# Self-attention of a decoder layer: value products of 130 columns, the output in five pieces, and one 16-bit copy of the exponentials made by VectorE

## The reference

```python
qn = _rmsnorm(q, q_gamma) * dh ** (-0.5)
kn = _rmsnorm(k, k_gamma)
sim = jnp.einsum('bhid,bhjd->bhij', qn, kn)
attn = jax.nn.softmax(sim, axis=-1)
out = jnp.einsum('bhij,bhjd->bhid', attn, v)
```

## Time and profile before

| what | value |
| --- | --- |
| runs, us | 2266.23, 2267.96, 2263.83; median 2266.23 |
| the profiled execution's own time | 2270.32 us |
| its span, first to last instruction | 2268.5 us |
| mean granted TensorE clock | 0.989 |
| instructions | 62703, of them 22392 matmuls |
| DMA | 65.24 MB in 102349 packets |

### The profile page before, as it was taken

One profiled execution on the slowest core, in us unless ns is written; L12 is line 12 of the kernel. 1 busy time (PEld: TensorE's weight loads), 2 busy tenths in 40 slices (PEclk: granted clock), 3 DMA queues, 4 the chain that ended last, 5 costly groups with the idle time before them and its releaser, 6 DMA issues. The chain is left out here.

```text
span 2268.5 us, 62703 instructions
## 1 busy us (share of the span) xinstructions
PE 2161.2 (95%) x22392; PEld 1243.8 (55%) x22392; DVE 1567.6 (69%) x2601; ACT 1606.2 (71%) x1831; POOL 1451.5 (64%) x1010
## 2 busy tenths in 40 slices
PE   6999999999997999999999999999999978998999
PEld 3545666666664455444445456666666644554444
DVE  6997777777776666753379977777777766677522
ACT  4557999999997566631146489999999965666210
POOL 3425889888887586721234178889888975866210
PEclk9999999999999999999999999999999999999999
DMA  5210000000002202102122100000000031020000
GB/s 108 65 42 1 11 0 9 9 9 9 9 9 63 64 2 48 38 21 73 43 63 64 28 2 10 9 0 9 9 9 9 10 89 38 2 62 24 20 24 33
DMA packets 102349, 65.24 MB, mean 29 GB/s; under 512 B 75346, under 2 KB 75346, under 8 KB 102226
## 3 DMA queue, kind: packets, MB, share of 16 engines
q1 hardware_dynamic: 102226, 63.57, 12.7%
HBM read 46.69 MB, written 8.39 MB: 24 GB/s over the span
## 5 line engine op out<-in xcount | busy, mean ns | idle before, releaser
L599 POOL TENSOR_TENSOR qkn<-wide 128x1024 f16<-128x1024 f32 x448 | 952.9, 2155 | 140.2 <-PE bank L716 124.1
L920 DVE TENSOR_REDUCE sq<-bank 128x1 f32<-128x512 f32 x1024 | 685.3, 688 | 216.3 <-PE bank L668 209.7
L845 ACT ACTIVATE wide<-bank,shift 128x1024 f32<-128x1024 f32 x512 | 571.4, 1116 | 14.5 <-POOL qkn L599 6.5
L837 ACT ACTIVATE wide<-bank,shift 128x1024 f16<-128x1024 f32 x512 | 569.1, 1112 | 9.1 <-PE bank L684 9.1
L683 PE MATMUL bank<-q_hh,ko 128*128 (+1 forms) x1024 | 388.7, 380 | 13.1 <-ACT wide L845 13.0
L668 PE MATMUL bank<-ko,q_hh 128*128 (+1 forms) x1024 | 386.8, 380 | 9.2 <-DVE sq L920 5.9
L684 PE MATMUL bank<-q_lm,k_h 65*128 (+1 forms) x1024 | 389.0, 380 | 0.0
L701 PEld LDWEIGHTS bank<-v_hl,wide 128*128 128x128 f16 x4096 | 287.6, 98 | 63.3 <-issue 5.6
L701 PE MATMUL bank<-v_hl,wide 128*128 (+1 forms) x4096 | 319.8, 192 | 0.1
L703 PE MATMUL bank<-v_hl,wide 128*128 (+1 forms) x4096 | 318.2, 193 | 0.0
L703 PEld LDWEIGHTS bank<-v_hl,wide 128*128 128x128 f16 x4096 | 267.5, 96 | 58.7
(11 more groups left out here) (227 smaller groups left out, 4177.4 us busy)
## 6 DMA issues: line engine op xcount, KB each, us to landing
wide<-in_x SPq DMA_DIRECT2D x32, 256.0 KB, 2.7
q_lm<-in_x SPq DMA_DIRECT2D x32, 256.0 KB, 3.2
ko<-in_L_ffn_W SPq DMA_DIRECT2D x32, 256.0 KB, 4.0
q_hh<-q_hh SPq DMA_DIRECT2D x32, 128.0 KB, 2.6
ko<-k_h SPq DMA_DIRECT2D x32, 128.0 KB, 2.8
out<-bo_b SPq DMA_DIRECT2D x16, 256.0 KB, 2.0
out<-xbo_b SPq DMA_DIRECT2D x16, 256.0 KB, 2.0
q_lm<-sq SPq DMA_DIRECT2D x248, 0.2 KB, 4.9
```

The lines of the kernel that those rows point to most:

```text
L599: pool.tensor_tensor(probs_l[:, p % 2, :], probs[:, p % 2, :], probs_h[:, p % 4, :], ALU.subtract).then_inc(pl_pool, 1)
L837: act.activation(probs_h[:, p % 4, :], SB[p % 2][:, :], ACT.Exp, bias=shift[:, 0:1]).then_inc(ph_ready, 1)
L845: act.activation(probs[:, p % 2, :], SB[p % 2][:, :], ACT.Exp, bias=shift[:, 0:1]).then_inc(p_ready, 1)
L920: dve.tensor_reduce(pm[:, s, k:k + 1], MB[k % 2], AX_X, ALU.max).then_inc(mx_free, 1)
```

## The change

It has three parts. (1) `values_high`: for three of the four query groups the products of 65 and of 64 columns become one of 130 columns; the spare column is filled with ones too, and a unit's result takes 3 x 130 + 65 columns of its bank: the part from the low columns of V stands beside the part from the high ones. The fourth group stays as it was. (2) `output`: in five steps, one behind each of the maxima 4 to 8. Step 0 is the reciprocal, step 1 the multiplication of the four high parts, steps 2 to 4 add, for one query group each, the low part times the reciprocal. (3) For pair 6, ACT makes the 32-bit exponential alone; VectorE makes `probs_h` from it by a `tensor_reduce` with maximum over an axis of one element, behind maximum 11 (behind number 9 in the first unit), and TensorE's high products and POOL's subtraction of that pair wait for it on a semaphore of its own, `ph_dve`. Left out below are the lines that make the semaphores `ph_dve` and `o_high`.

```diff
@@ -494,6 +496,8 @@
                     LA = 2
                     MAXED = UNITS - LA
                     AHEAD = 6
+                    CAST = 6
+                    WIDE = TPC - 1
                     vf = v_hl
                     next_h = {"o": share4[0], "xq": share4[1]}
                     next_l = {"o": share4[2], "xq": share4[3]}
@@ -584,7 +588,7 @@
 
                         pool.wait_ge(a_v_done, T0 + KB)
                         pool.nop(nofuse=True)
-                        pool.memset(v_hl[:, :].rearrange("p (k e) -> p k e", e=VW)[:, :, DH:DH + 1], 1.0)\
+                        pool.memset(v_hl[:, :].rearrange("p (k e) -> p k e", e=VW)[:, :, DH:DH + 2], 1.0)\
                             .then_inc(a_ones, 1)
                         pool.wait_ge(a_ones, (b + 1) * (KB + 1))
                         pool.nop(nofuse=True)
@@ -594,6 +598,10 @@
                                 if p == DVE_PAIR:
                                     continue
                                 pool.wait_ge(p_ready, G + p + 1)
+                                if p == CAST:
+
+                                    pool.wait_ge(ph_dve, U0 + u + 1)
+                                    pool.nop(nofuse=True)
 
                                 pool.wait_ge(lo_done, G + p + 1)
                                 pool.tensor_tensor(probs_l[:, p % 2, :], probs[:, p % 2, :], probs_h[:, p % 4, :],
@@ -685,7 +693,10 @@
                             mm.then_inc(s_ready, 1)
 
                         def values_high(u, p, ob):
-                            pe.wait_ge(ph_ready, (U0 + u) * PAIRS + p + 1)
+                            if p == CAST:
+                                pe.wait_ge(ph_dve, U0 + u + 1)
+                            else:
+                                pe.wait_ge(ph_ready, (U0 + u) * (PAIRS - 1) + (p if p < CAST else p - 1) + 1)
                             if isinstance(u, int) and u == 0 and p == 0:
 
                                 pe.wait_ge(a_v_ready, T0 + KB + 1)
@@ -697,11 +708,13 @@
                                 v0 = (2 * p + half) * (H * VW) + u // CH * VW
                                 for t in range(TPC):
                                     rows = probs_h[:, p % 4, half * CT + t * P:half * CT + t * P + P]
-                                    o0 = t * (DH + 1)
-                                    pe.matmul(ob[:, o0:o0 + DH + 1], rows, vf[:, bass.ds(v0, DH + 1)],
+                                    o0 = t * VW
+                                    wide = VW if t < WIDE else DH + 1
+                                    pe.matmul(ob[:, o0:o0 + wide], rows, vf[:, bass.ds(v0, wide)],
                                               start=(p == 0 and half == 0 and t == 0), stop=False, skip_group_check=True)
-                                    pe.matmul(ob[:, o0:o0 + DH], rows, vf[:, bass.ds(v0 + DH + 2, DH)],
-                                              start=False, stop=False, skip_group_check=True)
+                                    if t >= WIDE:
+                                        pe.matmul(ob[:, o0:o0 + DH], rows, vf[:, bass.ds(v0 + DH + 2, DH)],
+                                                  start=False, stop=False, skip_group_check=True)
 
                         def values_low(u, p, ob):
 
@@ -834,7 +847,9 @@
                             G = (U0 + u) * PAIRS
                             for p in range(PAIRS):
                                 act.wait_ge(s_ready, G + p + 1)
-                                act.activation(probs_h[:, p % 4, :], SB[p % 2][:, :], ACT.Exp, bias=shift[:, 0:1]).then_inc(ph_ready, 1)
+                                if p != CAST:
+                                    act.activation(probs_h[:, p % 4, :], SB[p % 2][:, :], ACT.Exp, bias=shift[:, 0:1])\
+                                        .then_inc(ph_ready, 1)
 
                                 if p - 2 == DVE_PAIR:
                                     act.wait_ge(pl_dve, U0 + u + 1)
@@ -926,6 +941,12 @@
                             dve.tensor_reduce(nm0[:, :, DH] if isinstance(r, int) and r == 0 else nm[:, s, :], pm[:, s, :].rearrange("p (a k) -> p a k", k=4), AX_X, ALU.max,
                                               negate=True).then_inc(nm_ready, 1)
 
+                        def probs_high(u):
+                            p = CAST
+                            dve.wait_ge(p_ready, (U0 + u) * PAIRS + p + 1)
+                            dve.tensor_reduce(probs_h[:, p % 4, :], probs[:, p % 2, :].rearrange("p (n a) -> p n a", a=1), AX_X,
+                                              ALU.max).then_inc(ph_dve, 1)
+
                         def probs_low(u):
                             p, G = DVE_PAIR, (U0 + u) * PAIRS + DVE_PAIR
                             dve.wait_ge(p_ready, G + 1)
@@ -938,15 +959,28 @@
                             first = u // (2 * CH) * (CH * TPC * P) + u % CH * (TPC * P) + u // CH % 2 * DH
                             return of[:, bass.ds(first, TPC * P)].rearrange("p (t d) -> p t d", d=P)[:, :, 0:DH]
 
-                        def output(u, s):
-
-                            o4 = OB[s][:, 0:TPC * (DH + 1)].rearrange("p (t e) -> p t e", e=DH + 1)
+                        def output(u, s, step):
+
+                            skip = s * (TPC * VW - CT)
+                            four = pairs[3][:, s * CT - skip:s * CT - skip + TPC * VW].rearrange("p (t e) -> p t e", e=VW)
                             r4 = rden[:, :].rearrange("p (t a) -> p t a", a=1)
-                            dve.wait_ge(lo_done, (U0 + u + 1) * PAIRS + 2)
-                            dve.reciprocal(r4, o4[:, :, DH:DH + 1]).then_inc(o_rec, 1)
-                            dve.wait_ge(o_rec, U0 + u + 1)
-                            dve.tensor_tensor(o_out(u), o4[:, :, 0:DH], r4.broadcast_to([P, TPC, DH]), ALU.mult)\
-                                .then_inc(o_free, 1)
+                            o_u = o_out(u)
+                            if step == 0:
+                                dve.wait_ge(lo_done, (U0 + u + 1) * PAIRS + 2)
+                                dve.reciprocal(r4, four[:, :, skip + DH:skip + DH + 1]).then_inc(o_rec, 1)
+                            elif step == 1:
+                                dve.wait_ge(o_rec, U0 + u + 1)
+                                dve.tensor_tensor(o_u, four[:, :, skip:skip + DH], r4.broadcast_to([P, TPC, DH]), ALU.mult)\
+                                    .then_inc(o_high, 1)
+                            else:
+                                t = step - 2
+                                if t == 0:
+                                    dve.wait_ge(o_high, U0 + u + 1)
+                                low = dve.scalar_tensor_tensor(
+                                    out=o_u[:, t, :], in0=OB[s][:, t * VW + DH + 2:(t + 1) * VW], scalar=rden[:, t:t + 1],
+                                    in1=o_u[:, t, :], op0=ALU.mult, op1=ALU.add)
+                                if t == WIDE - 1:
+                                    low.then_inc(o_free, 1)
 
                         def split_both(pieces):
 
@@ -966,10 +1000,12 @@
                             for k in range(16):
                                 if maxed:
                                     reduce_max(u + LA, k, s)
-                                if k == 4 and not first:
-                                    output(u - 1, 1 - s)
+                                if 4 <= k < 4 + 2 + WIDE and not first:
+                                    output(u - 1, 1 - s, k - 4)
                                 if k == (6 if first else 2 * DVE_PAIR + 1):
                                     probs_low(u)
+                                if k == (9 if first else 2 * CAST - 1):
+                                    probs_high(u)
                             if maxed:
                                 negate_max(u + LA, s)
 
@@ -994,7 +1030,8 @@
                         split_both(PIECES_P3[0:2])
                         unit(MAXED + 1, 1, maxed=False)
                         split_both(PIECES_P3[2:4])
-                        output(UNITS - 1, 1)
+                        for step in range(2 + WIDE):
+                            output(UNITS - 1, 1, step)
 
 
             with ExitStack() as mlp:
```

More of the change, by code:

```diff
@@ L227, in decoder_layer @@
         ph_ready = sem("ph_ready")
+        ph_dve = sem("ph_dve")
         p_ready = sem("p_ready")
@@ L236, in decoder_layer @@
         o_rec = sem("o_rec")
+        o_high = sem("o_high")
         o_free = sem("o_free")
```

## The result

The changed kernel takes 2262.4 us, median of 20 runs (2259.7 to 2265.2); the kernel before, on the same chips, 2267.0. The ratio is 0.9981, 95% interval 0.9974 to 0.9988: about 4.3 us won, where 12.6 were forecast. One of the 20 executions of the kernel before took 3674 us; neither the median nor the ratio rests on it. The profiled execution has 2265.2 us with a span of 2263.4, 5.1 less than before's.

What follows compares the result with a forecast made beforehand. TensorE, full in the steady part, bounds the kernel; a unit changes by -0.16 - 0.19 + 0.09 = -0.26 us, times 58 units -15, ends +2.4: 2266.2 - 12.6, about 2254 us. Range 2238 to 2272 us; faster 0.70.

Steps and rivals of the forecast that it cites:

- the edge of the loop: End of TensorE's loop pass: 0.12 us of a unit's 16.63, that is 0.24 once in two units.
- that slack: VectorE's maximum 12 before TensorE needs its bank: 0.24 us, less 0.1 and 0.06, about nothing left.
- product 14: TensorE waits there for VectorE, whose pair 4 subtraction overlaps POOL's: +0.09 us a unit, bounds 0 and 0.35.
- POOL's ring: POOL's six subtractions, an exponential, block 5 and hand-off: closes at 16.1 us plus pair 6's wait, just under TensorE.
- wide products: TensorE: 48 products of 130 columns at 58.0 ns replace pairs at 61.3 ns, -0.16 us a unit.
- The rival of loads that come to light: TensorE: a wide product pays its weight load after its columns, 85 ns; +0.95 us a unit, 2323 us; chance 0.04.
- Output in pieces: VectorE's waits for its own results fall under maxima, so TensorE's hole before product 7 goes: -0.19 us a unit.
- The copy: VectorE's one-element reduction for pair 6 lasts 1.22 us; floor 1.1, 2.6 with a cost per result.
- its two rivals: VectorE's copy: slow one-element axis (2310 or 2334 us, chance 0.10), or stretched by POOL (about 2298 us, chance 0.05).
- ACT's relief: ACT loses 1.0 us of 16 in a unit; nothing gained, since TensorE is what is full.
- Ends: First and last units of each sample: about +0.7 us twice and +0.5 twice, together +2.4 us.
- VectorE's queue is later: VectorE's hand-offs each cost 0.05 us more; saving 0 to 0.1 a unit, 2263 to 2269 us; chance 0.13.

Runs made afterwards that it cites:

- j: The changed kernel with TensorE's loop turned, so that its edge lies behind block 2 and not behind block 7: 2254.8 us, ratio 0.9947 to the kernel before.
- a: The changed kernel with the copy of pair 6 given back to ACT: 2254.9 us, ratio 0.9950 to the kernel before.
- b: The kernel before with only the copy of pair 6 by VectorE added: 2274.0 us, ratio 1.0029.
- o: The kernel before with the output in two steps and TensorE's loop turned, narrow products: 2253.6 us, ratio 0.9941.
- k: The changed kernel with the copy of pair 6 back on ACT and TensorE's loop turned: 2248.65 us, ratio 0.9915 to the kernel before.
- p: o with pair 0's subtraction moved from POOL to VectorE, six left on POOL: 2248.9 us, ratio 0.9917 to the kernel before.
- n: k with pair 0's subtraction moved from POOL to VectorE, six left on POOL: 2240.9 us, ratio 0.9883 to the kernel before.
- e: The kernel before with only the output cut in two, reciprocal behind maximum 4 and multiplication behind 5: 2256.7 us, ratio 0.9958.
- h: The changed kernel with pair 6's copy as a plain tensor_copy instead of the one-element reduction: 2305.3 us, ratio 1.0170 to the kernel before.
- d: The kernel before with four units in a pass of TensorE's and VectorE's loops: 2322.7 us, ratio 1.024.
- c: The changed kernel with four units in a pass of TensorE's and VectorE's loops: 2335.8 us, ratio 1.030 to the kernel before.

## Why the prediction was wrong, point by point

**The step that failed** is in "What bounds the kernel now": "the other 0.12 I put on the edge of the loop, which comes once in two units (0.24)". The sum then carried the edge as a constant. It isn't one: beside the gaps in the block behind it, about 0.3 us a pass in both kernels, an edge costs 0.66 us from the branch to the next product, less what is queued on TensorE at that moment. That second part went from 0.04 to 0.35 us a pass. j shows it: with the edge moved and nothing else it is 0.06, the period is 0.16 us shorter and the time 7.6 us. That the shorter queue comes from the sequencer's waits for maxima 12 and 13 behind the copy is read from their margins (0.93 to 0.09 and 0.18 us) and agrees with a and b, where copy and queue change together; maximum 12 moved by itself wasn't tried. It holds for the copy's share, 0.09 of the 0.16 us a unit; the cause of the share that a has too stays open. I had worked out that slack ("about nothing is left") and asked only whether product 14 would be late. The miss of a unit, 0.12 us, is 0.16 (edge) + 0.07 (POOL's ring) + 0.02 (hole before product 7) - 0.07 (wide products) - 0.06 (product 14): the edge is more than all of it. Two terms that came out better than forecast hide part of the three that came out worse.

**POOL's ring**, "just under TensorE", is just over it once blocks are short: +0.07 a unit in the account, and the table of o, k, p, n shows that it eats about two thirds of the wide products' gain.

**Wide products**: -0.16 forecast, -0.23 measured; 56.7 ns (56.3 in the rows shown) lies between my 58.0 and the lower bound. The rival of loads that come to light (2323 us) falls. The Trainium skill's formula for a product by itself (TensorE: Matmul & The Clock Gate, Back-to-back issue gap), N/2.4 + 2.5 = 56.7, agrees with the rows; its 81 ns at 128 columns for a stream with weight loads doesn't hold here.

**Output in pieces**: -0.19 forecast, -0.17 measured, hole gone in e as well. The small additions take 0.27 us and not 0.2, without effect.

**Product 14**: +0.09 forecast, +0.03 measured. **The copy**: 1.22 us, as forecast; its two rivals fall for the one-element reduction. POOL doesn't stretch it, as the Trainium skill has it (GPSIMD Engine Reference, Specifications). h shows a form that is stretched; that it is one of the 2-port mode, which the sentence names, no trace here says. **ACT's relief**: nothing, as forecast. **Ends**: +2.4 forecast, +2.7 measured.

The time, 2262.4, lies inside the range of 2238 to 2272, which is wide, and near the foot of the rival "VectorE's queue is later" (2263 to 2269). That rival named a stall of product 14 that isn't there, so it was not right either. The sign was right, and the four priced terms in the main; that the edge grows was never priced, POOL's ring was called hidden, and the two took two thirds of the gain.

## What to carry to other kernels

A wait that ends just in time for the array can be late for the sequencer, as it was here: ask what is queued behind it, and above all whether a branch of the loop follows within a few products, where the queue is what hides the branch. Place loop edges after stretches without close waits. When a stage has two bounds within 0.1 us of each other, price an edit to the one by the other's ring, and relieve both in one step.

## What the hardware did unexpectedly

- The edge of a loop on TensorE: 0.66 us from branch to next product, nearly the same in all kernels here with two units a pass (medians 0.66 to 0.74), hidden only by queued products, and wider gaps in the block behind it (0.27 us a pass before the change). At four units a pass 4.0 us (d) and 4.2 (c), with 2.3 and 2.1 MB more of instruction traffic.
- A reduction over a one-element axis converts 1024 elements of 32 bits in 1.22 us beside POOL without contention; the plain copy swings between 0.82 and 2.00 us, and POOL waits for it.
